# Expert slot tiles: the chosen expert's weights copied to fixed places by VectorE and ScalarE, and held stationary by TensorE

## The chip, the cores and the metric

The kernel runs on one core of a Trainium2 chip. The metric is the device time of one execution in microseconds; a kernel's time is the median of its runs. TensorE multiplies matrices, VectorE (DVE), ScalarE (ACT) and GpSimd (POOL) work elementwise, SyncE (SP) issues most transfers. Each engine has a queue of its own and works through it in order; semaphores tie the queues together.

## The reference

One block of a network, on x of 16 x 512 rows of 128 values: a modulated layer norm, a gather convolution whose result is added to x, a second modulated layer norm, and a mixture of 8 experts of which each row takes 2. The change touches only the experts:

```python
scores = jnp.einsum('btd,ed->bte', x, gate_w)
topk_scores, topk_idx = jax.lax.top_k(scores, TOP_K)       
topk_probs = jax.nn.softmax(topk_scores, axis=-1)
h12 = jnp.einsum('btd,ehd->bteh', x, w12)
h1, h2 = (h12[..., :H], h12[..., H:])
hidden = jax.nn.silu(h1) * h2
expert_out = jnp.einsum('bteh,edh->bted', hidden, w3)
y = jnp.sum(total_probs[..., None] * expert_out, axis=-2)
```

All data are float32.

## The kernel before

The kernel has two long stages. In the first (to about 1048 us) the convolution runs over 512 tiles, and each row's two experts are chosen. Each row, with its target and its gate, is scattered by GpSimd into a table in DRAM in which every expert has its own region, filled up to whole tiles of 128 rows. A table of tiles (`whichi`: the expert of each slot tile; `wherei`: where its rows stand) is worked out by VectorE.

The second stage runs over `SLOT_TILES` = 135 slot tiles, each of 128 rows of one expert. For tile j:

- SyncE loads the rows to `xt` (a ring of 12), L451.
- TensorE `slots_turned(j)` turns them, L1122, and VectorE `slots_out(j)` copies the result to `xT` (2 buffers), L1434.
- TensorE `hidden(j)`, L1128: one product with `xT` stationary and the expert's 512 columns of `w12` moving, read at an address that a register gives. The rows of the slot tile are the partitions of the result `ps_h`.
- ScalarE `silu(j)`, L852, on the first 256 columns; VectorE `hidden(j)`, L1440, multiplies by the other 256 and writes `hid`.
- TensorE `hidden_turned(j)`, L1135: two transposes, since the second product needs the inner dimension on the partitions; ScalarE `hidden_out(j)`, L858, copies them out to `hidT`.
- TensorE `second(j)`, L1143: two products (halves of the inner 256) with `hidT` stationary and the expert's `w3` moving, at an address from a register; each float32 product is two instructions.
- ScalarE `rows_out(j)`, L865, multiplies by the gate; VectorE `targets(j)`, L1447, converts the target indices; GpSimd scatters the rows to DRAM, L704, over a ring of 4.

The order is written out by hand. TensorE goes through `slots_turned(j + 2)`, `hidden(j + 1)`, `hidden_turned(j)`, `second(j - 1)`; VectorE through `slots_out(j + 2)`, `hidden(j + 1)`, `targets(j)`; ScalarE through `silu(j + 1)`, `hidden_out(j)`, `rows_out(j - 1)`. Nearly all buffers between them are double. Once in four tiles TensorE's queue (and SyncE's, for `wherei`) loads four numbers from SBUF into registers, L1154 (L445): one load instruction, then register arithmetic and an assertion for each number. After the last tile each row's two expert rows are fetched, added and stored with x.

Of the kernel before, what the change touches and what calls it, by code (L numbers as in the profile page):

```python
# [4 lines left out]
B, L, C = 16, 512, 128  # L5
HEADS, D, TAPS, BINS = 8, 16, 32, 64
P = 128
# [21 lines left out]
EXPERTS, FF = 8, 256  # L29
HALVES = FF // P  # L30
# [3 lines left out]
SLOT_TILES = ASSIGNED // P + EXPERTS - 1  # L34
SPARE = EXPERTS - 1
ROW = C + 2
XRING = 12
YRING = 4
EPS = 1e-5
MAX_FREQ, MIN_FREQ = 16.0, 1.0  # L40

# [51 lines left out]
def build(nc, x, wave_wT, wave_b, kern_wT, kern_b, out_wT, w12T, w3T, gateT, cT, wmod,  # L93
          c_n, c_p, c_e, c_tok, c_ident, c_iota, c_tri, c_id, c_trash, c_tile, out):
    fp32, bf16, i32, u32 = mybir.dt.float32, mybir.dt.bfloat16, mybir.dt.int32, mybir.dt.uint32
    ALU, ACT, AX = mybir.AluOpType, mybir.ActivationFunctionType, mybir.AxisListType
# [20 lines left out]
    with ctx:  # L117
        def sb(name, shape, dt=fp32):
            return ctx.enter_context(nc.sbuf_tensor(name, shape, dt))

        def pb(name):
            return ctx.enter_context(nc.psum_tensor(name, [P, 512], fp32))

        def sem(name):
            return ctx.enter_context(nc.semaphore(name))
# [5 lines left out]
        ident = sb("ident", [P, P])  # L131
# [75 lines left out]
        spots = sb("spots", [P, TOP, RES])  # L207
# [11 lines left out]
        whichi = sb("whichi", [P, SLOT_TILES + 1], i32)  # L219
# [7 lines left out]
        w12 = flat[:, 0:EXPERTS * 2 * FF]  # L227
        w3 = hgr[:, PAIRS % 2, :]
        xt = dl[:, :, :, :, :].rearrange("p s j h k -> p (s j h k)")[:, 0:XRING * ROW].rearrange("p (s n) -> p s n", s=XRING)
        zrow = att[:, :, :].rearrange("p a n -> p (a n)")[:, 0:EXPERTS * ROW].rearrange("p (e n) -> p e n", n=ROW)  # L230
        xT = ee[:, 0, 0:2 * P].rearrange("p (s n) -> p s n", s=2)
        sh = ee[:, 1, :].rearrange("p (s n) -> p s n", s=2)
        hid = aw[:, 0, 0:512].rearrange("p (s n) -> p s n", s=2)
        hidT = aw[:, 1, 0:512].rearrange("p (s n) -> p s n", s=2)
        yrow = aw[:, 2, 0:YRING * P].rearrange("p (s n) -> p s n", s=YRING)
        idu = sb("idu", [P, XRING], u32)
        y1 = att[:, 0:4, :].rearrange("p a n -> p (a n)").rearrange("p (s n) -> p s n", s=2)
# [5 lines left out]

        ps = [pb(f"ps{n}") for n in range(8)]
        ps_n, ps_p, ps_t, ps_y, side = ps[0:2], ps[2:4], ps[4:6], ps[6], ps[7]
        ps_x, ps_h, ps_u, ps_z = ps[0:2], ps[2:4], ps[4:6], ps[6:8]

        s_const, s_mod, s_modst, s_modld = sem("consts_loaded"), sem("mod_done"), sem("mod_stored"), sem("mod_loaded")
        s_silu, s_modps, s_zero = sem("silu_done"), sem("mod_product"), sem("edges_zeroed")
# [22 lines left out]
        s_w, s_spare, s_pad2, s_tab = sem("expert_weights_loaded"), sem("spare_filled"), sem("pad_spots_ready"), sem("tile_table_ready")  # L272
# [1 line left out]
        s_zrow = sem("zero_rows_ready")  # L274
        s_xt = [sem(f"slots_loaded{n}") for n in range(XRING)]
        s_xp, s_xe, s_hp, s_si, s_hid = sem("slots_turned"), sem("slots_evicted"), sem("hidden_product"), sem("silu_ready"), sem("hidden_ready")
        s_up, s_ue, s_zp, s_ze, s_idu = sem("hidden_turned"), sem("hidden_evicted"), sem("expert_product"), sem("expert_rows"), sem("targets_ready")
        s_ys = [sem(f"expert_scattered{n}") for n in range(YRING)]
        s_xf = [sem(f"pair_fetched{n}") for n in range(2)]
        s_xm = sem("kept_rows_loaded")  # L280
# [14 lines left out]
        def _(sp):  # L295
# [176 lines left out]
            for j in range(SLOT_TILES):  # L472
                slots_in(j)
                if j >= 2 * XRING and j - 2 * XRING < PAIRS:
                    kept_in(j - 2 * XRING)
            for n in range(YRING):
                sp.wait_ge(s_ys[n], 16 * len(range(n, SLOT_TILES, YRING)))
            fetch(0, 0)
# [9 lines left out]
        def _(pool):  # L488
            pool.memset(power[:, :], -0.5)
            pool.memset(middle[:, :], MIN_FREQ + (MAX_FREQ - MIN_FREQ) / 2)  # L490
            pool.memset(tiny[:, :], EPS)
            pool.memset(zeros, 0.0).then_inc(s_set, 1)
# [215 lines left out]
        def _(act):  # L708
# [100 lines left out]
            for T in range(NT):  # L809
                i, R, r, h = T // TILES, T // HEADS, T // HEADS % RES, T % HEADS  # L810
                last, more = i - 1, i + 1 < PAIRS
# [36 lines left out]
            def silu(j):  # L848
                act.wait_ge(s_hp, j + 1)
                if j >= 2:  # L850
                    act.wait_ge(s_hid, j - 1)
                act.activation(sh[:, j % 2, :], ps_h[j % 2][:, 0:FF], ACT.Silu).then_inc(s_si, 1)  # L852

            def hidden_out(j):
                act.wait_ge(s_up, j + 1)
                if j >= 2:
                    act.wait_ge(s_zp, j - 1)
                act.activation(hidT[:, j % 2, :], ps_u[j % 2][:, 0:FF], ACT.Copy).then_inc(s_ue, 1)  # L858

            def rows_out(j):  # L860
                s, y = j % XRING, j % YRING
                act.wait_ge(s_zp, j + 1)
                if j >= YRING:
                    act.wait_ge(s_ys[y], 16 * (j // YRING))
                act.activation(yrow[:, y, :], ps_z[j % 2][:, 0:C], ACT.Identity, scale=xt[:, s, C + 1:C + 2]).then_inc(s_ze, 1)  # L865

            silu(0)
            for j in range(SLOT_TILES):
                if j + 1 < SLOT_TILES:
                    silu(j + 1)  # L870
                hidden_out(j)
                if j:
                    rows_out(j - 1)
            rows_out(SLOT_TILES - 1)

        @block.tensor
        def _(pe):
# [188 lines left out]
            for T in range(NT):  # L1066
                i, R, r, h = T // TILES, T // HEADS, T // HEADS % RES, T % HEADS
                last, more = i - 1, i + 1 < PAIRS
# [54 lines left out]

            def hidden(j):
                pe.wait_ge(s_xe, j + 1)
                if j >= 2:
                    pe.wait_ge(s_hid, j - 1)
                nc.tensor.matmul(ps_h[j % 2][:, :], xT[:, j % 2, :], w12[:, bass.ds(experts[j % 8] * (2 * FF), 2 * FF)], start=True, stop=True).then_inc(s_hp, 1)  # L1128

            def hidden_turned(j):  # L1130
                pe.wait_ge(s_hid, j + 1)
                if j >= 2:
                    pe.wait_ge(s_ue, j - 1)
                for k in range(HALVES):
                    last = nc.tensor.transpose(ps_u[j % 2][:, k * P:k * P + P], hid[:, j % 2, k * P:k * P + P], ident[:, :])  # L1135
                last.then_inc(s_up, 1)

            def second(j):
                pe.wait_ge(s_ue, j + 1)
                if j >= 2:  # L1140
                    pe.wait_ge(s_ze, j - 1)
                for k in range(HALVES):
                    last = nc.tensor.matmul(ps_z[j % 2][:, 0:C], hidT[:, j % 2, k * P:k * P + P], w3[:, bass.ds(experts[j % 8] * (HALVES * C) + k * C, C)],  # L1143
                                            start=(k == 0), stop=(k == HALVES - 1))
                last.then_inc(s_zp, 1)

            experts = [None] * 8
            pe.wait_ge(s_tab, 1)
            pe.wait_ge(s_w, 32)
            pe.wait_ge(s_rk, PAIRS)  # L1150
            for j in range(-2, SLOT_TILES + 1):
                if (j + 2) % 4 == 0 and j + 2 < SLOT_TILES:
                    n = (j + 2) % 8
                    experts[n:n + 4] = nc.values_load_multi_w_load_instructions(whichi[0:1, j + 2:j + 6], engines=(mybir.EngineType.PE,),  # L1154
                                                                                min_val=0, max_val=EXPERTS - 1)[1]
                if j + 2 < SLOT_TILES:
                    slots_turned(j + 2)
                if 0 <= j + 1 < SLOT_TILES:
                    hidden(j + 1)
                if 0 <= j < SLOT_TILES:  # L1160
                    hidden_turned(j)
                if 0 <= j - 1 < SLOT_TILES:
                    second(j - 1)

        @block.vector
        def _(dve):
            n = [0]
# [175 lines left out]
            for T in range(NT):  # L1343
                i, R, r, h = T // TILES, T // HEADS, T // HEADS % RES, T % HEADS
                last, more = i - 1, i + 1 < PAIRS
# [68 lines left out]
            for k, d in enumerate((1, 2, 4)):  # L1414
                a, b = upto[:, k % 2, :], upto[:, 1 - k % 2, :]
# [14 lines left out]
            def slots_out(j):  # L1430
                dve.wait_ge(s_xp, j + 1)
                if j >= 2:
                    dve.wait_ge(s_hp, j - 1)
                nc.vector.tensor_copy(xT[:, j % 2, :], ps_x[j % 2][:, 0:P]).then_inc(s_xe, 1)  # L1434

            def hidden(j):
                dve.wait_ge(s_si, j + 1)
                if j >= 2:
                    dve.wait_ge(s_up, j - 1)
                nc.vector.tensor_tensor(hid[:, j % 2, :], sh[:, j % 2, :], ps_h[j % 2][:, FF:2 * FF], ALU.mult).then_inc(s_hid, 1)  # L1440

            def targets(j):
                s = j % XRING
                dve.wait_ge(s_xt[s], 16 * (j // XRING + 1))
                if j >= XRING:
                    dve.wait_ge(s_ys[j % YRING], 16 * ((j - XRING) // YRING + 1))
                nc.vector.tensor_copy(idu[:, s:s + 1], xt[:, s, C:C + 1]).then_inc(s_idu, 1)  # L1447

            slots_out(0)
            slots_out(1)  # L1450
            hidden(0)
            for j in range(SLOT_TILES):
                if j + 2 < SLOT_TILES:
                    slots_out(j + 2)
                if j + 1 < SLOT_TILES:
                    hidden(j + 1)
                targets(j)

            dve.wait_ge(s_xm, 16 * (3 * PAIRS - 1))
            for f in range(PAIRS):  # L1460
                s = f % 2
# [78 lines left out]
```

## Time and profile before

| | us |
|---|---|
| median of 3 runs | 1399.45 (1394.16 to 1401.42) |
| the profiled execution | 1404.66 |
| its span, first to last instruction | 1402.9 |
| TensorE matmuls busy over the span | 1131.3 (81%) |
| VectorE | 1037.9 (74%) |
| ScalarE | 931.3 (66%) |
| GpSimd | 711.3 (51%) |
| slot tiles: first slot transpose to last scatter | 1088.6 to 1353 |

Times in the profile are microseconds from the span's start, durations of single instructions often ns. PE is a matmul, PEld a weight load of TensorE, and a name with q at its end (PEldq, DVEq, ACTq) is the queue that feeds the engine: register work and waits are done there and are not counted as busy. "issue" is idle time for which the profile knows no other engine. The busy shares over the whole span say little here, since the two stages have different limits; the slot tiles are read by themselves.

### The profile page before, as it was taken

The page shows a single profiled execution, that of the slowest core. Times are in us where ns is not written, and L with a number is a line of the kernel's source. Part 1 is how long each engine was busy: PE and PEld are TensorE (multiplying, and loading weights), DVE is VectorE, ACT ScalarE, POOL GpSimd, SP SyncE. Part 2 cuts the span into 40 slices and gives each one's busy share as a digit, 9 for nine tenths or more (in the row PEclk, how much of TensorE's full clock was granted, in tenths as well). Part 3 has the DMA queues.
Part 4 walks back from the last instruction along what each step waited for, and adds up shares of the span by engine and source line. Part 5 has one row for each costly group of instructions (what it writes and reads, how often), then busy time and mean ns, then how long its engine had stood idle before and what let it go on. Part 6 is the DMA issues. An engine that isn't in the chain of part 4 may idle for free. (4 is left out here: it accounts for less than half of the span.)

```text
span 1402.9 us, 34813 instructions
## 1 busy us (share of the span) xinstructions
PE 1131.3 (81%) x11182; PEld 781.2 (56%) x11339; DVE 1037.9 (74%) x2314; ACT 931.3 (66%) x1905; POOL 711.3 (51%) x906
## 2 busy tenths in 40 slices
PE   0569998998999999899999989999930899999940
PEld 0346666665666666566666666666630565555530
DVE  1379899989989999998999999889933333333336
ACT  0268888788788878878887888788800455555530
POOL 4335227447745844854683584544336344545430
PEclk9989999999999999999999999999965899999975
DMA  4345445545544554554554455445511262222237
GB/s 160 112 127 151 140 105 157 154 127 152 154 125 133 171 135 129 156 146 115 171 149 124 133 143 135 140 133 136 155 57 42 73 191 71 71 71 73 67 119 266
DMA packets 213344, 181.27 MB, mean 129 GB/s; under 512 B 147632, under 2 KB 183344, under 8 KB 212272
## 3 DMA queue, kind: packets, MB, share of 16 engines
q1 hardware_dynamic: 204496, 161.12, 41.3%
q0 software_dynamic: 8672, 17.92, 3.8%
q8 instruction: 96, 1.57, 0.5%
q14 instruction: 80, 0.66, 0.2%
HBM read 96.86 MB, written 82.12 MB: 128 GB/s over the span
## 5 line engine op out<-in xcount | busy, mean ns | idle before, releaser
L774 ACT ACTIVATE ee<-ps,f 128x512 f32<-128x512 f32 x512 | 354.7, 693 | 120.1 <-remote 67.1
L1291 DVE TENSOR_TENSOR aw<-dq,ks 128x520 f32<-128x520 int32 x512 | 418.2, 817 | 2.2 <-DMA ks<-k_scratch 2.2
L1281 DVE SCALAR_TENSOR_TENSOR dq<-ps,ee 128x512 int32<-128x512 f32 x512 | 350.4, 684 | 45.4 <-PE ps L978 38.6
L986 PE MATMUL ps<-ident,aw 128*128 128x128 f32 x2048 | 314.6, 276 | 39.9 <-ACT att L782 22.5
L986 PEld LDWEIGHTS ps<-ident,aw 128*128 128x128 f32 x2048 | 239.0, 141 | 184.6 <-issue 66.2
L782 ACT ACTIVATE att<-ps 128x512 f32<-128x512 f32 x512 | 310.3, 606 | 20.7 <-PE ps L986 18.2
L978 PE MATMUL ps<-cn,ptt 128*128 128x512 bf16 x512 | 195.3, 382 | 28.3 <-issue 12.1
L614 POOL COPY kn<-kn 128x256 f32<-128x256 f32 x64 | 25.5, 398 | 348.9 <-DVE kn L1271 343.9
L704 POOL DMA_INDIRECT y_scratch<-aw,idu x135 | 129.6, 960 | 135.9 <-ACT aw L865 124.4
L583 POOL DMA_INDIRECT slot_scratch<-hrow,spotu x128 | 139.7, 1092 | 44.5 <-issue 33.4
L1440 DVE TENSOR_TENSOR aw<-ee,ps 128x256 f32<-128x256 f32 x135 | 56.9, 422 | 136.0 <-ACT ee L852 113.2
L852 ACT ACTIVATE ee<-ps 128x256 f32<-128x256 f32 x135 | 51.9, 384 | 156.7 <-PE ps L1128 144.2
L1128 PE MATMUL ps<-kn,ee 128*128 x270 | 143.5, 614 | 0.0
L1006 PE MATMUL ps<-att,dl 128*32 128x128 f32 x4096 | 138.4, 276 | 0.1
L973 PE MATMUL ps<-cp,ptt 128*128 128x512 bf16 x355 | 136.8, 385 | 0.2 <-issue 0.2
L1006 PEld LDWEIGHTS ps<-att,dl 128*32 128x32 f32 x4096 | 104.1, 109 | 21.7 <-ACT att L789 8.5
L993 PE MATMUL ps<-ident,ka 128*128 128x128 f32 x512 | 78.4, 276 | 17.0 <-POOL ka L628 15.9
L1122 PE MATMUL ps<-ident,dl 128*128 128x128 f32 x135 | 38.5, 285 | 60.7 <-issue 58.6
L621 POOL TENSOR_TENSOR kd<-kn 128x504 f32<-128x504 f32 x64 | 87.0, 1360 | 0.0
L789 ACT ACTIVATE att<-ps 128x512 f32<-128x512 f32 x128 | 77.2, 603 | 13.6 <-PE ps L993 13.5
L1143 PE MATMUL ps<-hgr,aw 128*128 x540 | 82.6, 275 | 0.2
L1135 PEld LDWEIGHTS ps<-ident,aw 128*128 128x128 f32 x270 | 38.2, 142 | 71.9 <-issue 62.1
(174 smaller groups left out, 1693.7 us busy)
## 6 DMA issues: line engine op xcount, KB each, us to landing
k_scratch<-kn SPq DMA_DIRECT2D x64, 512.0 KB, 3.4
ka<-e_scratch SPq DMA_DIRECT2D x64, 512.0 KB
ks<-k_scratch SPq DMA_DIRECT2D x128, 130.0 KB
e_scratch<-kr SPq DMA_DIRECT2D x128, 126.0 KB
dl<-slot_scratch SPq DMA_DIRECT2D x135, 65.0 KB
att<-y_scratch SPq DMA_DIRECT2D x16, 512.0 KB, 5.3
xc<-in_x SPq DMA_DIRECT2D x8, 512.0 KB, 5.9
h_scratch<-hx SPq DMA_DIRECT2D x16, 256.0 KB, 4.1
```

The costliest lines, as they stand in the source:

```text
L583: pool.indirect_dma_start(out=slots[:, :], out_offset=bass.IndirectOffsetOnAxis(ap=spotu[:, k * RES + r:k * RES + r + 1], axis=0), in_=hro ...
L621: pool.tensor_tensor(kd[:, R % 2, :].rearrange("p (h k) -> p h k", k=EDGES), k[:, :, LO:LO + EDGES], k[:, :, LO + 1:LO + BINS], ALU.subtra ...
L704: pool.indirect_dma_start(out=yscr[:, :], out_offset=bass.IndirectOffsetOnAxis(ap=idu[:, s:s + 1], axis=0), in_=yrow[:, y, :], in_offset=N ...
L774: act.activation(ee[:, T % ERING, :], ps_p[T % 2][:, :], ACT.Relu, scale=f27[:, i % 2, r, h:h + 1]).then_inc(s_e, 1)
L782: act.activation(att[:, h, :], ps_t[UNIT["tile", T] % 2][:, :], ACT.Copy).then_inc(s_ev, 1)
L973: nc.tensor.matmul(ps_p[T % 2][:, :], params_of(T), cp[:, T % QUAD, :], start=True, stop=True).then_inc(s_p, 1)
L978: nc.tensor.matmul(ps_n[T % 2][:, :], params_of(T), cn[:, T % QUAD, :], start=True, stop=True).then_inc(s_n, 1)
L986: last = nc.tensor.transpose(bank[:, j * P:j * P + P], aw[:, T % RING, o:o + P], ident[:, :])
L1006: last = nc.tensor.matmul(ps_y[ROWS * k:ROWS * k + ROWS, g * P:g * P + P], dl[:, R // RES % 2, j, h, :], att[:, h, j * P:j * P + P], start ...
L1128: nc.tensor.matmul(ps_h[j % 2][:, :], xT[:, j % 2, :], w12[:, bass.ds(experts[j % 8] * (2 * FF), 2 * FF)], start=True, stop=True).then_inc ...
L1281: nc.vector.scalar_tensor_tensor(dq[:, T % DRING, o:o + 512], ps_n[T % 2][:, :], SCALE, ee[:, T % ERING, :], ALU.mult, ALU.add).then_inc(s ...
L1291: nc.vector.tensor_tensor(aw[:, T % RING, :].rearrange("p (g k) -> p g k", k=8), dq[:, T % DRING, :].rearrange("p (g k) -> p g k", k=8), r ...
```

## The change

`w12c` (2 buffers of 512 columns) and `w3c` (2 of 256) are fixed places in SBUF. VectorE copies the tile's 512 columns of `w12` to the one (`first_weights`), ScalarE its 256 columns of `w3` to the other (`second_weights`). TensorE's `hidden` is now four products of 128 columns, each with a 128x128 block of `w12c` stationary and `xT` moving, so the result comes out with the inner dimension on the partitions. `hidden_turned` and `hidden_out` are gone; VectorE writes `hidT` (now 3 buffers) itself. The register loads move from TensorE's queue to VectorE's and ScalarE's.

The diff shows ScalarE first, then TensorE, then VectorE.

```diff
...
-            def hidden_out(j):
-                act.wait_ge(s_up, j + 1)
+            def second_weights(j):
+                if j % 4 == 0:
+                    spots[:] = nc.values_load_multi_w_load_instructions(whichi[0:1, j:j + 4], engines=(mybir.EngineType.Activation,),
+                                                                        min_val=0, max_val=EXPERTS - 1)[1]
                 if j >= 2:
                     act.wait_ge(s_zp, j - 1)
-                act.activation(hidT[:, j % 2, :], ps_u[j % 2][:, 0:FF], ACT.Copy).then_inc(s_ue, 1)
+                act.activation(w3c[:, j % 2, :], w3[:, bass.ds(spots[j % 4] * (HALVES * C), HALVES * C)], ACT.Copy).then_inc(s_w3, 1)
...
-            silu(0)
-            for j in range(SLOT_TILES):
+            act.wait_ge(s_tab, 1)
+            act.wait_ge(s_w, 32)
+            for j in range(-1, SLOT_TILES + 1):
                 if j + 1 < SLOT_TILES:
+                    second_weights(j + 1)
                     silu(j + 1)
-                hidden_out(j)
-                if j:
+                if j >= 1:
                     rows_out(j - 1)
-            rows_out(SLOT_TILES - 1)
...
             def hidden(j):
                 pe.wait_ge(s_xe, j + 1)
+                pe.wait_ge(s_w12, j + 1)
                 if j >= 2:
                     pe.wait_ge(s_hid, j - 1)
-                nc.tensor.matmul(ps_h[j % 2][:, :], xT[:, j % 2, :], w12[:, bass.ds(experts[j % 8] * (2 * FF), 2 * FF)], start=True, stop=True).then_inc(s_hp, 1)
+                for k in range(2 * HALVES):
+                    last = nc.tensor.matmul(ps_h[j % 2][:, k * P:k * P + P], w12c[:, j % 2, k * P:k * P + P], xT[:, j % 2, :], start=True, stop=True)
+                last.then_inc(s_hp, 1)
...
             def second(j):
-                pe.wait_ge(s_ue, j + 1)
+                pe.wait_ge(s_hid, j + 1)
+                pe.wait_ge(s_w3, j + 1)
                 if j >= 2:
                     pe.wait_ge(s_ze, j - 1)
                 for k in range(HALVES):
-                    last = nc.tensor.matmul(ps_z[j % 2][:, 0:C], hidT[:, j % 2, k * P:k * P + P], w3[:, bass.ds(experts[j % 8] * (HALVES * C) + k * C, C)],
+                    last = nc.tensor.matmul(ps_z[j % 2][:, 0:C], hidT[:, j % HRING, k * P:k * P + P], w3c[:, j % 2, k * C:k * C + C],
...
-                if (j + 2) % 4 == 0 and j + 2 < SLOT_TILES:
-                    n = (j + 2) % 8
-                    experts[n:n + 4] = nc.values_load_multi_w_load_instructions(whichi[0:1, j + 2:j + 6], engines=(mybir.EngineType.PE,),
-                                                                                min_val=0, max_val=EXPERTS - 1)[1]
                 if j + 2 < SLOT_TILES:
                     slots_turned(j + 2)
                 if 0 <= j + 1 < SLOT_TILES:
                     hidden(j + 1)
-                if 0 <= j < SLOT_TILES:
-                    hidden_turned(j)
                 if 0 <= j - 1 < SLOT_TILES:
                     second(j - 1)
...
+            def first_weights(j):
+                if j % 4 == 0:
+                    spots_of[:] = nc.values_load_multi_w_load_instructions(whichi[0:1, j:j + 4], engines=(mybir.EngineType.DVE,),
+                                                                           min_val=0, max_val=EXPERTS - 1)[1]
+                if j >= 2:
+                    dve.wait_ge(s_hp, j - 1)
+                nc.vector.tensor_copy(w12c[:, j % 2, :], w12[:, bass.ds(spots_of[j % 4] * (2 * FF), 2 * FF)]).then_inc(s_w12, 1)
+
             def hidden(j):
                 dve.wait_ge(s_si, j + 1)
-                if j >= 2:
-                    dve.wait_ge(s_up, j - 1)
-                nc.vector.tensor_tensor(hid[:, j % 2, :], sh[:, j % 2, :], ps_h[j % 2][:, FF:2 * FF], ALU.mult).then_inc(s_hid, 1)
+                if j >= HRING:
+                    dve.wait_ge(s_zp, j - HRING + 1)
+                nc.vector.tensor_tensor(hidT[:, j % HRING, :], sh[:, j % 2, :], ps_h[j % 2][:, FF:2 * FF], ALU.mult).then_inc(s_hid, 1)
...
-            slots_out(0)
-            slots_out(1)
-            hidden(0)
-            for j in range(SLOT_TILES):
+            dve.wait_ge(s_tab, 1)
+            dve.wait_ge(s_w, 32)
+            for j in range(-2, SLOT_TILES):
                 if j + 2 < SLOT_TILES:
+                    first_weights(j + 2)
                     slots_out(j + 2)
-                if j + 1 < SLOT_TILES:
+                if 0 <= j + 1 < SLOT_TILES:
                     hidden(j + 1)
-                targets(j)
+                if j >= 0:
+                    targets(j)
```

## Rows read from the trace of the kernel before

**Rows 1.** Stretches: length; busy us (instructions) by engine; PEclk; DMA; GB/s.

```profile
60.00:100.00 40.00, 27.05 (x194) 16.53 (x197) 24.69 (x52) 23.74 (x45) 11.56 (x22) 0.87 0.52 135
1150.00:1330.00 180.00, 163.53 (x847) 106.67 (x846) 66.91 (x282) 96.38 (x282) 90.34 (x95) 1.00 0.26 72
```

**Rows 2.** Chain of waits in the slot tiles: start us, us, what.

```profile
1202.59 0.11 PE ps L1122
1202.69 0.86 PE ps L1128 x2
1203.56 0.22 PE ps L1135 x2
1203.77 0.45 PE ps L1143 x4
1204.22 0.64 issue
1204.86 0.30 PE ps L1122
1205.16 1.05 PE ps L1128 x2
```

**Rows 3.** Register load on TensorE's queue, all, then one; the next weights.

```profile
L1154 PEldq TENSOR_LOAD <-whichi x34: 327/331/518, 1065.2 to 1340.7; - x34
...
L1154 PEldq FUSED_REGOPS  x4: 146/148/151, 1211.3 to 1212.2; - x4
L1154 PEldq SEQ_ASSERT  x4: 18/18/18, 1211.5 to 1212.4; - x4
L1154 PEldq TENSOR_LOAD <-whichi x1: 329/329/329, 1210.9 to 1210.9; - x1
...
1212.52 0.14 PEld L1122 LDWEIGHTS ps<-ident,dl 128*128 128x128 f32 x1 [0.92 <-issue]
```

**Rows 4.** Timeline of the slot tiles: start us, us, engine, line, operation.

```profile
1201.96 0.38 ACT L852 ACTIVATE ee<-ps 128x256 f32<-128x256 f32 x1 [0.60 <-issue]
1201.98 0.61 PE L1143 MATMUL ps<-hgr,aw 128*128 x4
1202.24 0.38 ACT L858 ACTIVATE aw<-ps 128x256 f32<-128x256 f32 x1
...
1202.38 0.42 DVE L1440 TENSOR_TENSOR aw<-ee,ps 128x256 f32<-128x256 f32 x1 [0.95 <-ACT ee L852]
...
1202.53 1.02 PE L1128 MATMUL ps<-kn,ee 128*128 x2
...
1202.71 0.15 DVE L1447 CAST idu<-dl 128x1 uint32<-128x1 f32 x1
1202.78 0.28 DVE L1434 COPY ee<-ps 128x128 f32<-128x128 f32 x1
...
1203.59 0.39 ACT L852 ACTIVATE ee<-ps 128x256 f32<-128x256 f32 x1 [0.60 <-PE ps L1128]
```

**Rows 5.** One-input VectorE work in SBUF, by line, then timeline beside a scatter.

```profile
L1409 DVE TENSOR_SCALAR fill<-filli 128x8 f32<-128x8 int32 x1 | 0.2, 172 | 0.0
...
1064.19 0.96 POOL L583 DMA_INDIRECT slot_scratch<-hrow,spotu  x1 [0.30 <-issue]
1064.22 0.23 DVE L1426 TENSOR_SCALAR which<-which 128x136 f32<-128x136 f32 x1
1064.75 0.43 DVE L1428 CAST wherei<-where 128x136 int32<-128x136 f32 x1
```

**Rows 6.** Semaphore waits on ScalarE's and VectorE's queues, 1150 to 1300 us.

```profile
L851 ACTq EVENT_SEMAPHORE  x79: 17/17/17, 1151.1 to 1299.6; - x79
L1439 DVEq EVENT_SEMAPHORE  x79: 21/21/21, 1152.1 to 1299.7; - x79
```

**Rows 7.** Timeline, GpSimd: one scatter of a row of them, idle time before.

```profile
1078.11 0.96 POOL L698 DMA_INDIRECT slot_scratch<-att,padu  x1 [0.30 <-issue]
```

More of the change, by code:

```diff
@@ L38 @@
 YRING = 4
+HRING = 3
 EPS = 1e-5
@@ L232, in build @@
         sh = ee[:, 1, :].rearrange("p (s n) -> p s n", s=2)
-        hid = aw[:, 0, 0:512].rearrange("p (s n) -> p s n", s=2)
-        hidT = aw[:, 1, 0:512].rearrange("p (s n) -> p s n", s=2)
+        hidT = aw[:, 0:2, :].rearrange("p a n -> p (a n)")[:, 0:HRING * FF].rearrange("p (s n) -> p s n", s=HRING)
+        w12c = ee[:, 2:4, :]
+        w3c = kr[:, :, :].rearrange("p s n -> p (s n)")[:, 0:2 * HALVES * C].rearrange("p (s n) -> p s n", s=2)
         yrow = aw[:, 2, 0:YRING * P].rearrange("p (s n) -> p s n", s=YRING)
@@ L245, in build @@
         ps_n, ps_p, ps_t, ps_y, side = ps[0:2], ps[2:4], ps[4:6], ps[6], ps[7]
-        ps_x, ps_h, ps_u, ps_z = ps[0:2], ps[2:4], ps[4:6], ps[6:8]
+        ps_x, ps_h, ps_z = ps[0:2], ps[2:4], ps[6:8]
         s_const, s_mod, s_modst, s_modld = sem("consts_loaded"), sem("mod_done"), sem("mod_stored"), sem("mod_loaded")
@@ L276, in build @@
         s_xp, s_xe, s_hp, s_si, s_hid = sem("slots_turned"), sem("slots_evicted"), sem("hidden_product"), sem("silu_ready"), sem("hidden_ready")
-        s_up, s_ue, s_zp, s_ze, s_idu = sem("hidden_turned"), sem("hidden_evicted"), sem("expert_product"), sem("expert_rows"), sem("targets_ready")
+        s_w12, s_w3, s_zp, s_ze, s_idu = sem("first_weights_copied"), sem("second_weights_copied"), sem("expert_product"), sem("expert_rows"), sem("targets_ready")
         s_ys = [sem(f"expert_scattered{n}") for n in range(YRING)]
@@ L852, in silu @@
                 act.activation(sh[:, j % 2, :], ps_h[j % 2][:, 0:FF], ACT.Silu).then_inc(s_si, 1)
-            def hidden_out(j):
-                act.wait_ge(s_up, j + 1)
+            spots = [None] * 4
+            def second_weights(j):
+                if j % 4 == 0:
+                    spots[:] = nc.values_load_multi_w_load_instructions(whichi[0:1, j:j + 4], engines=(mybir.EngineType.Activation,),
+                                                                        min_val=0, max_val=EXPERTS - 1)[1]
                 if j >= 2:
                     act.wait_ge(s_zp, j - 1)
-                act.activation(hidT[:, j % 2, :], ps_u[j % 2][:, 0:FF], ACT.Copy).then_inc(s_ue, 1)
+                act.activation(w3c[:, j % 2, :], w3[:, bass.ds(spots[j % 4] * (HALVES * C), HALVES * C)], ACT.Copy).then_inc(s_w3, 1)
             def rows_out(j):
@@ L1125, in hidden, with second @@
                 pe.wait_ge(s_xe, j + 1)
+                pe.wait_ge(s_w12, j + 1)
                 if j >= 2:
                     pe.wait_ge(s_hid, j - 1)
-                nc.tensor.matmul(ps_h[j % 2][:, :], xT[:, j % 2, :], w12[:, bass.ds(experts[j % 8] * (2 * FF), 2 * FF)], start=True, stop=True).then_inc(s_hp, 1)
-            def hidden_turned(j):
+                for k in range(2 * HALVES):
+                    last = nc.tensor.matmul(ps_h[j % 2][:, k * P:k * P + P], w12c[:, j % 2, k * P:k * P + P], xT[:, j % 2, :], start=True, stop=True)
+                last.then_inc(s_hp, 1)
+            def second(j):
                 pe.wait_ge(s_hid, j + 1)
-                if j >= 2:
[L1133 to L1138, printed above, removed]
-                pe.wait_ge(s_ue, j + 1)
+                pe.wait_ge(s_w3, j + 1)
                 if j >= 2:
@@ L1142, in second @@
                 for k in range(HALVES):
-                    last = nc.tensor.matmul(ps_z[j % 2][:, 0:C], hidT[:, j % 2, k * P:k * P + P], w3[:, bass.ds(experts[j % 8] * (HALVES * C) + k * C, C)],
+                    last = nc.tensor.matmul(ps_z[j % 2][:, 0:C], hidT[:, j % HRING, k * P:k * P + P], w3c[:, j % 2, k * C:k * C + C],
                                             start=(k == 0), stop=(k == HALVES - 1))
                 last.then_inc(s_zp, 1)
-            experts = [None] * 8
-            pe.wait_ge(s_tab, 1)
-            pe.wait_ge(s_w, 32)
             pe.wait_ge(s_rk, PAIRS)
             for j in range(-2, SLOT_TILES + 1):
-                if (j + 2) % 4 == 0 and j + 2 < SLOT_TILES:
-                    n = (j + 2) % 8
-                    experts[n:n + 4] = nc.values_load_multi_w_load_instructions(whichi[0:1, j + 2:j + 6], engines=(mybir.EngineType.PE,),
-                                                                                min_val=0, max_val=EXPERTS - 1)[1]
                 if j + 2 < SLOT_TILES:
@@ L1434, in slots_out @@
                 nc.vector.tensor_copy(xT[:, j % 2, :], ps_x[j % 2][:, 0:P]).then_inc(s_xe, 1)
+            spots_of = [None] * 4
+            def first_weights(j):
[5 more added lines that the diff above has]
+                nc.vector.tensor_copy(w12c[:, j % 2, :], w12[:, bass.ds(spots_of[j % 4] * (2 * FF), 2 * FF)]).then_inc(s_w12, 1)
             def hidden(j):
                 dve.wait_ge(s_si, j + 1)
-                if j >= 2:
-                    dve.wait_ge(s_up, j - 1)
-                nc.vector.tensor_tensor(hid[:, j % 2, :], sh[:, j % 2, :], ps_h[j % 2][:, FF:2 * FF], ALU.mult).then_inc(s_hid, 1)
+                if j >= HRING:
+                    dve.wait_ge(s_zp, j - HRING + 1)
+                nc.vector.tensor_tensor(hidT[:, j % HRING, :], sh[:, j % 2, :], ps_h[j % 2][:, FF:2 * FF], ALU.mult).then_inc(s_hid, 1)
             def targets(j):
```

## The prediction

> **What bounds the kernel now.** I first read the page's slices for stages. The last quarter of the span but for its end is a stage of its own: TensorE almost full, VectorE mostly idle. That is the loop over the 135 slot tiles, the only part the change touches. In its middle 180 us [rows 1] TensorE is busy 163.53 us (91%), with its clock granted in full (1.00, so the 2.4 GHz level); ScalarE 54%, VectorE 37%, GpSimd 50%. So TensorE bounds the stage, and what it does in each tile is the price list.
>
> The chain of waits gives that list [rows 2]: after the slot transpose (L1122, issued every 0.11 us) come 0.86 us of the wide product (L1128), 0.22 of two transposes back (L1135), 0.45 of the second product (L1143, four instructions, thus 0.112 each): 1.64 us a tile. Once in four tiles stands "issue", 0.64 us, followed by a slower start (0.30 and 1.05 where 0.11 and 0.86 are usual). This is the loading of four expert numbers into registers (L1154): the load instruction starts at 1210.9, and the next weights go in at 1212.52, 1.62 us later [rows 3]. It began while older matmuls still ran, hence only some 1.1 us show. From one load to the last one there are 17 groups in 1340.7 - 1210.9 = 129.8 us: **7.64 us for four tiles**, 1.91 each. Everything below is compared with this 7.64; there are 135/4 = 33.75 groups.
>
> **The change part by part.** *TensorE, throughput.* The wide product of 0.86 becomes four products of 128 columns. Each one is two instructions, as in L1143, so 8 x 0.112 = 0.90 us. The two transposes (0.22) go, and so does the register load (1.1 per group). A tile needs 0.11 + 0.90 + 0.45 = 1.46 us; if TensorE stayed the bound, a group took 5.84 us.
>
> *ScalarE.* It drops the eviction of the transposed rows (L858, 128x256, next instruction 0.28 us later) and gains a copy of the same 128x256 from SBUF. No row has that exact copy; between 0.24 and 0.34, I take 0.28 as the nearest [rows 4]. Busy time is unchanged, but the *order* is new. The copy for tile k waits for the second product of tile k-2 (its buffer), and the silu of tile k is queued right behind it. TensorE runs that second product after the hidden product of tile k. So silu(k), which now starts 0.04 us after its own product's end (1202.53 + 1.02 to 1203.59, [rows 4]), would then also wait for 0.45 us of other matmuls and a copy.
>
> *VectorE.* It gains a 128x512 f32 copy from SBUF. The nearest rows: in SBUF a one-input operation took 231 ns for 136 elements (L1426), against 172 for 8 (L1409), so 0.46 ns an element [rows 5]. That gives 172 + 504 x 0.46 = 404 ns; I take 0.40 from its start to the next one. At the slope of two-input work (0.33 for 256, L1440) it would be 0.60, the upper bound; 0.30 is the lower one. The copy for k+2 is queued behind hid(k), the product with the gate, and ahead of the transposed slots of k+2, and TensorE needs both of these before H(k+2).
>
> These two queues close a **loop** over two tiles. Its terms, with starts to next starts from [rows 4] and [rows 2], the first worked out above: H(k) 0.90; second product of k-2 0.45, its drain 0.16 (0.61 in the timeline less 0.45); hand-over to ScalarE 0.04; weight copy 0.28; silu 0.38; hand-over 0.04; hid(k) 0.33; targets 0.07; copy of the first weights 0.40; slots out 0.29; hand-over to TensorE 0.04 (taken like the others). Sum **3.38 us for two tiles**, 1.69 each. So TensorE with its 1.46 is no longer the bound even without any load; a group is 6.76 us.
>
> *The register load, moved.* Both VectorE and ScalarE now do it once in four tiles. On ScalarE it follows the scaled rows of k-3, and silu(k) waits anyway for a product that VectorE's own load has held up; more than 1.6 us of waiting covers it, and I cost it at nothing. If that cover were gone, it would show once per group as on VectorE. On VectorE it has no cover: it stands between targets and the weight copy, inside the loop. The queue runs ahead of the engine, so the load starts when hid(k) is released, about 0.15 us after it (two waits, two instructions); without a load the copy would start 0.33 + 0.07 = 0.40 after it. Its own length: 1.62 on TensorE's queue. VectorE's queue is slower: the same semaphore instruction takes 21 ns there against 17 on ScalarE's [rows 6]. With that ratio on all but the 0.33 of the load proper, 0.33 + 1.29 x 1.24 = 1.93. I take 1.85, nearer to the row of its own queue. Exposed: 0.15 + 1.85 - 0.40 = **1.60 us per group**; bounds 0.9 (a load of 1.15, the bare sum of the instructions' times in [rows 3], 0.33 + 4 x 0.166 = 0.99, plus some dispatch) and 2.0.
>
> The Trainium skill (Advanced Engine Details and Errata, Clock Domains) gives VectorE's sequencer 0.96 GHz and the others 1.2 GHz; the 21 and 17 ns agree with it. By that rule alone the load would be 1.62 x 1.25 = 2.03 us and the forecast some 6 us longer; the sum above rests on the rows.
>
> **Sum.** A group: 2 x 3.38 + 1.60 = 8.36 us against 7.64, so 0.72 x 33.75 = 24.3 us more. The profiled execution took 1404.66 us (span 1402.9 and what lies around it), so it would take 1429; this execution was 5 above the median of the three runs, 1399.45, and from that median the forecast is 1399.45 + 24.3 = **1424 us**. Nothing ahead of the stage changes: the first slot transpose waits for the scatters, which follow each other every 1.26 us until after 1078 [rows 7], while TensorE's first load stands at 1065.2 [rows 3], behind its wait for the weights: they are there, and the first copies will be. Break-even is an exposed load of 7.64 - 6.76 = 0.88 us.
>
> GpSimd's scatter needs 0.96 + 0.30 = 1.26 us [rows 7], under 2.1 a tile, so it has room. The DMA queues see the same transfers.
>
> **The rivals.**
> (a) *The load costs little on VectorE.* With 0 exposed a group takes 6.76, so -30 us: 1370; with 0.4 it is 1383. For: nobody has measured it on that queue. Against: [rows 3], and the load has no cover of more than 0.4. 0.12.
> (b) *TensorE remains the bound* (group 5.84): -61 us, 1339. For: 91% busy today. Against: silu(k) stands behind a wait for a product that TensorE runs later. It needs the loop's terms to be some 14% shorter and no load. 0.05.
> (c) *The copy of the first weights runs at one element per cycle* (0.60 instead of 0.40): twice 0.20 in each group's loop, +13.5 us: 1437. It decides if the rate of [rows 5] doesn't hold for a copy whose source address is in a register. 0.12.
> (d) *The copy and the scatter get in each other's way* in SBUF. L1428, 136 elements, took 0.43 us where L1426 took 0.23; it ended 0.03 after the scatter that had begun at 1064.19, while L1426 ran inside the same scatter undisturbed [rows 5]. If each copy in the loop loses that 0.20, +13.5 us: 1437. If it waits for half a scatter of 0.96, 0.48 x 2 x 33.75 = +32 us: 1456. 0.11 in all.
> The Trainium skill (SBUF - State Buffer, Who interferes with whom) says that a VectorE copy of this kind and a GpSimd instruction hold a shared port for their whole length, the second one fully blocked. That is the case with 1456; L1426's undisturbed 0.23 speaks against it, L1428's 0.43 for a part of it.
> (e) *TensorE's clock falls.* It would be busy 1.46 of 2.09 us, 70%. In 60 to 100 us of the span it was 68% busy and the clock granted was 0.87 [rows 1]. By that, a quarter of the time at the lower level adds some 0.39 to the 1.51 us of TensorE in the loop: +26 us, 1450. Pauses of over 0.6 us exist today at a full clock. 0.06.
>
> **How the numbers follow.** The forecast 0.49; (a) 0.12, (b) 0.05, (c) 0.12, (d) 0.11, (e) 0.06; the loop as said but the exposed load near break-even (0.7 to 1.1) 0.05. A measurement of this kernel can tell about 0.5%, 7 us, from no change. Faster by more than that: (a) and (b), 0.17. Within it: the last case and the short end of the forecast, 0.10. Slower: 0.73. The forecast's own range is 1400 to 1440: the load's bounds give -24 and +13, the two copies' lower ends -6 and -3. The range for 8 in 10 reaches over (c), most of (d) and (e), down to the near end of (a): 1392 to 1450.
>
> **What would show it.** In the profile after: TensorE about 70% busy in the stage; a group of four tiles 8.4 us long, with intervals between hidden products that alternate (about 1.46 and 1.92) and one of about 3.5; silu's idle time ended by the weight copy's wait, thus by the second product; VectorE's copy at 0.43; L1154's load gone from TensorE's queue and one of 1.8 to 2.0 us on VectorE's. Wrong if silu starts at its own product's end, if the copy takes 0.7 or varies with the scatter, if the idle time of TensorE is under 10%, or if the granted clock is under 1.

## The result, and the profile after

| | before | after |
|---|---|---|
| median of 4 runs each, us (before: the three above and one more) | 1400.06 | 1433.96 (1427.91 to 1435.38) |
| the profiled execution, us | 1404.66 | 1434.57 |
| slot tiles, first to last scatter, us | 253.7 | 288.5 |

The changed kernel is slower: ratio 1.0255, 95% interval 1.0223 to 1.0287. On another chip, that of the second set of experiments below, the kernel before took 1378 us and the changed one 1.0216 times as long (1.0199 to 1.0233). The slot tiles (start of the first scatter to start of the last: 1098.73 to 1352.40 before, 1093.55 to 1382.05 after) took 34.8 us more. The two profiled executions lie 29.9 us apart, since the stage ahead of the slot tiles ended some 5 us earlier in the second one; what made it do so stays open. On the other chip the kernel before with a short load and the changed kernel reach their first scatter at nearly the same time (1073.7 and 1074.3 us), so it doesn't look like a part of the change.

The same stretch as in [rows 1], of the kernel after: length; busy us (instructions) of PE, PEld, DVE, ACT, POOL; granted clock; DMA; GB/s.

```profile
1150.00:1330.00 180.00, 136.38 (x1080) 126.22 (x1079) 87.70 (x336) 78.74 (x250) 89.44 (x84) 0.97 0.22 63
```

TensorE fell from 163.53 to 136.38 us of the 180, and no other engine is above half. So no engine's own work fills the stage, and the waits have to be read. The longest waits of 1150 to 1350 us say which (engine and line, what it waited for: us in total, times, the longest):

```profile
ACT kr L865 <- PE ps L1146: 111.1, 88, 4.4
...
DVE aw L1445 <- ACT ee L854: 72.5, 68, 3.2
```

The first is ScalarE's copy of the second weights (L865) waiting for the second product (L1146); the silu (L854) behind it has no idle time of its own. That is the wait that the forecast named. The timeline lets the loop be read off, from one hidden product (L1137) to the next but one:

```profile
1199.80 1.16 PE L1137 MATMUL ps<-ee 128*128 128x128 f32 x8 [1.69 <-issue]
...
1200.80 0.61 PE L1146 MATMUL ps<-kr,aw 128*128 128x128 f32 x4
...
1201.35 1.06 PE L1137 MATMUL ps<-ee 128*128 128x128 f32 x8
1201.54 0.42 ACT L865 ACTIVATE kr<-hgr 128x256 f32 x1 [2.46 <-PE ps L1146]
1201.86 0.37 ACT L854 ACTIVATE ee<-ps 128x256 f32<-128x256 f32 x1
...
1202.26 0.42 DVE L1445 TENSOR_TENSOR aw<-ee,ps 128x256 f32<-128x256 f32 x1 [1.46 <-ACT ee L854]
...
1202.60 0.15 DVE L1452 CAST idu<-dl 128x1 uint32<-128x1 f32 x1
...
1202.66 0.42 DVE L1439 COPY ee<-kn 128x512 f32 x1
1202.76 1.15 POOL L706 DMA_INDIRECT y_scratch<-aw,idu  x1 [2.38 <-DVE idu L1452]
...
1202.99 0.28 DVE L1428 COPY ee<-ps 128x128 f32<-128x128 f32 x1
...
1203.33 1.16 PE L1137 MATMUL ps<-ee 128*128 128x128 f32 x8 [0.37 <-DVE ee L1428]
```

1199.80 to 1203.33 is 3.53 us for two tiles. The next round holds VectorE's register load; here the copy of the first weights (L1439) comes 1.72 us after hid (L1445) instead of 0.40:

```profile
1204.88 1.06 PE L1137 MATMUL ps<-ee 128*128 128x128 f32 x8
...
1205.79 0.42 DVE L1445 TENSOR_TENSOR aw<-ee,ps 128x256 f32<-128x256 f32 x1 [1.06 <-ACT ee L854]
...
1207.51 0.43 DVE L1439 COPY ee<-kn 128x512 f32 x1 [1.23 <-issue]
...
1208.18 1.16 PE L1137 MATMUL ps<-ee 128*128 128x128 f32 x8 [1.69 <-issue]
```

From 1199.80 to 1208.18 is a group of four tiles: **8.38 us**. The load itself, on VectorE's queue (shortest, median and longest duration in ns; first and last start):

```profile
L1435 DVEq FUSED_REGOPS  x4: 183/186/190, 1206.3 to 1207.1; - x4
L1435 DVEq SEQ_ASSERT  x4: 23/23/23, 1206.5 to 1207.3; - x4
L1435 DVEq TENSOR_LOAD <-whichi x1: 345/345/345, 1205.9 to 1205.9; - x1
```

One more thing differs from before: stretches at TensorE's lower clock level. Two neighbouring windows of 10 us, and from the chain of waits the eight matmuls of a hidden product (0.89 us at the full clock, when nothing holds them up) in such a stretch:

```profile
1190.00:1200.00 10.00, 7.94 (x53) 7.46 (x54) 4.09 (x18) 3.79 (x12) 3.88 (x4) 0.84 0.20 55
1200.00:1210.00 10.00, 7.94 (x68) 7.47 (x68) 5.00 (x20) 3.87 (x13) 4.66 (x5) 1.00 0.23 66
```

```profile
1189.82 2.07 PE ps L1137 x8
```

### The profile page after: what moved, and what is told of

Same layout as the page of the kernel before. It is cut to its first block, busy times and chain, and to the rows that moved or that the text cites. A ratio compares the mean times of both kernels' runs of the same rounds, so it can differ in the third digit from the quotient of the medians.

```text
span 1432.8 us, 36095 instructions
## 1 busy us (share of the span) xinstructions
PE 1136.2 (79%) x11879; PEld 835.3 (58%) x11879; DVE 1082.1 (76%) x2449; ACT 919.3 (64%) x1905; POOL 726.0 (51%) x906
## 4 chain that ended last, share of the span: by engine, by line
PE 47%; issue 13%; DVE 10%; ACT 5%; POOL 4%; DMA 2%; DVEq 1%; SPq 1%; another core or an unknown queue 1%; ACTq 0%; POOLq 0%
PE ps L993 9%; PE ps L1137 9%; PE ps L1013 5%; PE ps L980 5%; DVE aw L1285 4%; PE ps L985 4%; PE ps L1146 3%; PE ps L1000 2%; PE ps L1035 2%; PE ps L947 2%; PE ps L1023 2%; DMA att<-y_scratch 2%; DVE dq L1275 1%; ACT att L784 1%; ACT ee L776 1%
## 5 line engine op out<-in xcount | busy, mean ns | idle before, releaser
L993 PEld LDWEIGHTS ps<-ident,aw 128*128 128x128 f32 x2048 | 239.5, 141 | 182.7 <-issue 66.3
L706 POOL DMA_INDIRECT y_scratch<-aw,idu x135 | 143.0, 1059 | 156.8 <-DVE idu L1452 130.5
L1137 PE MATMUL ps<-ee 128*128 128x128 f32 x1080 | 157.2, 291 | 68.4 <-issue 44.0
L980 PE MATMUL ps<-cp,ptt 128*128 128x512 bf16 x512 | 197.3, 386 | 0.0
L1137 PEld LDWEIGHTS ps<-ee 128*128 128x128 f32 x1080 | 138.2, 200 | 84.6 <-issue 55.1
L865 ACT ACTIVATE kr<-hgr 128x256 f32 x135 | 56.2, 416 | 178.1 <-PE ps L1146 158.0
L1445 DVE TENSOR_TENSOR aw<-ee,ps 128x256 f32<-128x256 f32 x135 | 56.6, 419 | 111.6 <-ACT ee L854 109.2
L1439 DVE COPY ee<-kn 128x512 f32 x135 | 60.1, 445 | 43.3 <-issue 43.3
L1146 PE MATMUL ps<-kr,aw 128*128 128x128 f32 x540 | 84.8, 281 | 0.9 <-ACT aw L872 0.9
```

The lines of the kernel that those rows point to most:

```text
L706: pool.indirect_dma_start(out=yscr[:, :], out_offset=bass.IndirectOffsetOnAxis(ap=idu[:, s:s + 1], axis=0), in_=yrow[:, y, :], in_offset=N ...
L980: nc.tensor.matmul(ps_p[T % 2][:, :], params_of(T), cp[:, T % QUAD, :], start=True, stop=True).then_inc(s_p, 1)
L993: last = nc.tensor.transpose(bank[:, j * P:j * P + P], aw[:, T % RING, o:o + P], ident[:, :])
L1137: last = nc.tensor.matmul(ps_h[j % 2][:, k * P:k * P + P], w12c[:, j % 2, k * P:k * P + P], xT[:, j % 2, :], start=True, stop=True)
L1146: last = nc.tensor.matmul(ps_z[j % 2][:, 0:C], hidT[:, j % HRING, k * P:k * P + P], w3c[:, j % 2, k * C:k * C + C], start=(k == 0), stop=( ...
```

## The experiments

My theory: two lengthenings put the loop above TensorE's work, ScalarE's order (silu behind the weight copy, thus behind another tile's second product) and VectorE's register load, which has no cover. The rivals: the copies and GpSimd's scatters hold each other up; the eight products are the bound; the clock.

They ran in two sets, on two chips. The first set holds the runs without VectorE's load, without ScalarE's load, with silu first and with the shorter load on VectorE; the second set holds the changed kernel and the last three. Each is compared with the kernel before on its own chip (1378.32 us in the first set, 1377.87 in the second). Differences to the changed kernel, for runs of the first set, go by way of these two, which agree within 0.5 us.

### The changed kernel on another chip

> The changed kernel as it is, on the chip of these runs. Its slot stage took 288.4 us from first to last scatter in the first profile, 34.7 more than before: 25 by the longer groups (8.38 against 7.64) and about 10 by stretches with the TensorE clock at its lower level. If those stretches belong to the kernel: 34 over the kernel before again. If they belong to that chip or execution: 24 to 27 over it.

Measured: 1407.89 us, 30.0 over before, ratio 1.0216 (1.0199 to 1.0233). That is between the two answers. (The changed kernel ran on the chip of the second set only, not on that of the first.) The profile still shows lowered stretches, but fewer, for instance:

```profile
1190.00:1200.00 10.00, 7.95 (x56) 7.71 (x56) 3.84 (x16) 3.41 (x11) 4.21 (x4) 0.83 0.22 56
```

Of the ten-microsecond windows from 1080 to 1350 two are under 1.00 here. In the first profile six windows from 1130 to 1350 are at 0.93 or lower. Its slot stage is 282.6 us (1074.3 to 1356.9), 5.9 less than there, with the same 8.38 for an undisturbed group.

### Without VectorE's register load

```diff
-                if j % 4 == 0:
-                    spots_of[:] = nc.values_load_multi_w_load_instructions(whichi[0:1, j:j + 4], engines=(mybir.EngineType.DVE,), ...
...
-                nc.vector.tensor_copy(w12c[:, j % 2, :], w12[:, bass.ds(spots_of[j % 4] * (2 * FF), 2 * FF)]) ...
+                nc.vector.tensor_copy(w12c[:, j % 2, :], w12[:, 0:2 * FF]) ...
```

> Leaves out VectorE's register loads: every tile's first weights are copied from expert 0's place, at a fixed address; the amount copied is the same. Loop theory (two tiles of ScalarE's and VectorE's queues bound the stage, the load is exposed 1.32 us once in four tiles): a group of four falls from 8.38 to 7.06 us, 45 us less than the changed kernel (1434), so 1389; if the groups at a lowered TensorE clock also go, up to 10 less, 1379. Rival, the scatter and the copies hold each other up: the copies stay, so at most 10 us are won, 1424. Rival, the eight products of TensorE are the bound: no change, 1434.

Measured: 1361.94 us, 16.4 under before (ratio 0.9883, 0.9866 to 0.9899), thus 46 under the changed kernel; 45 had been expected from the load alone. The timeline:

```profile
1202.31 1.16 PE L1137 MATMUL ps<-ee 128*128 128x128 f32 x8 [0.35 <-DVE ee L1428]
...
1205.84 1.16 PE L1137 MATMUL ps<-ee 128*128 128x128 f32 x8 [0.36 <-DVE ee L1428]
...
1209.36 1.16 PE L1137 MATMUL ps<-ee 128*128 128x128 f32 x8 [0.35 <-DVE ee L1428]
```

Every round is now 3.53 or 3.52 us, a group 7.05. All copies were still there, and the products too. So the copies and the eight products by themselves don't make the kernel slower than before; it took the load on top. "Silu first", below, shows that it took the order on ScalarE as well: without either one, the kernel is faster than before.

### Without ScalarE's register load

```diff
-                if j % 4 == 0:
-                    spots[:] = nc.values_load_multi_w_load_instructions(whichi[0:1, j:j + 4], engines=(mybir.EngineType.Activation,), ...
...
-                act.activation(w3c[:, j % 2, :], w3[:, bass.ds(spots[j % 4] * (HALVES * C), HALVES * C)], ACT.Copy) ...
+                act.activation(w3c[:, j % 2, :], w3[:, 0:HALVES * C], ACT.Copy) ...
```

> Leaves out ScalarE's register loads: every tile's second weights are copied from expert 0's place. Loop theory: the load is hidden behind ScalarE's wait for the second product, so no change, 1434 within 5. Rival, it is exposed like VectorE's: 1.3 x 33.75 = 44 us less, 1390.

Measured: 1401.73 us, 23.4 over before (1.0175, 1.0158 to 1.0192); the changed kernel is 30.0 over it, so 6 to 7 us were won and not 44. In this order of the queue the load is hidden. Most of the little that was won is another term: with a fixed address the copy starts 0.04 us after the second product's end (1201.91 + 0.61 to 1202.56) instead of 0.13 (1200.80 + 0.61 to 1201.54 above).

```profile
1201.91 0.61 PE L1143 MATMUL ps<-kr,aw 128*128 128x128 f32 x4
```

```profile
1202.56 0.42 ACT L862 ACTIVATE kr<-hgr 128x256 f32<-128x256 f32 x1 [2.08 <-PE ps L1143]
```

Its hidden products at 1200.92 and 1209.17 are one group apart, 8.25 us; 0.13 less in 33.5 groups is 4.4 us, and the slot stage is 4.5 us shorter than that of the changed kernel (278.1 against 282.6). The other 2 us are within the noise of the two comparisons.

### Silu first

```diff
                 if j + 1 < SLOT_TILES:
-                    second_weights(j + 1)
                     silu(j + 1)
+                    second_weights(j + 1)
```

> Only the order on ScalarE: silu(j + 1) ahead of the copy of the second weights of j + 1. Loop theory: silu no longer waits for the second product, 0.61 + 0.13 + 0.32 us leave the loop of two tiles; TensorE's 1.46 and VectorE's load are left, a group takes about 6.9 instead of 8.38, 49 us less than the changed kernel, 1385 (1375 if the clock stays up), under the kernel before. Rivals (copies and scatter in each other's way, eight products slow): 1420 or more.

Measured: 1357.61 us, 20.7 under before (0.9858, 0.9841 to 0.9874) and about 50 under the changed kernel, where 49 was expected. Two lines changed places, and a kernel slower than before became one 1.4% faster:

```profile
1199.91 1.16 PE L1137 MATMUL ps<-ee 128*128 128x128 f32 x8 [0.58 <-DVE ee L1428]
...
1201.46 1.06 PE L1137 MATMUL ps<-ee 128*128 128x128 f32 x8
...
1202.91 1.06 PE L1137 MATMUL ps<-ee 128*128 128x128 f32 x8
...
1204.52 1.16 PE L1137 MATMUL ps<-ee 128*128 128x128 f32 x8
...
1206.82 1.16 PE L1137 MATMUL ps<-ee 128*128 128x128 f32 x8 [0.59 <-DVE ee L1428]
```

A group is 6.91 us. The loop of 3.53 is gone (1.55, 1.45, 1.61), and one interval of 2.30 is left in a group. VectorE's load stands in it, but not alone. With silu ahead of it, ScalarE's load (L861) has lost its cover: the chain of waits of this kernel runs through both loads. In this order of the queue ScalarE's load delays its weight copy, thus the scaled rows (L872) and the next silu (L854), and by them the hid behind which VectorE's own load starts:

```profile
1201.46 0.15 ACTq L861
...
1202.14 0.15 ACTq L861
...
1202.79 0.26 ACT aw L872
1203.05 0.37 ACT ee L854
...
1204.52 0.35 DVEq L1435
```

How much of the 6.91 each load makes wasn't measured by itself; with both of them short, in the last experiment, a group is 5.80.

### A shorter load on VectorE

```diff
                     spots_of[:] = nc.values_load_multi_w_load_instructions(whichi[0:1, j:j + 4], engines=(mybir.EngineType.DVE,),
-                                                                           min_val=0, max_val=EXPERTS - 1)[1]
+                                                                           min_val=0, max_val=EXPERTS - 1,
+                        skip_runtime_bounds_check_because="which is clamped to EXPERTS - 1 and starts at 0")[1]
```

> VectorE's register loads without the bounds assertions, so with less register arithmetic behind the load instruction; all else as in the changed kernel. Loop theory with the length in the arithmetic (4 x 0.3 us of 1.6): the exposed part falls from 1.3 to 0.4 to 0.6, a group to 7.5 to 7.7, 23 to 30 us less, 1404 to 1411. Rival, the length is in the load instruction and its latency: under 8 us less. Rival theories without the load in the loop: 1434.

Measured: 1367.8 us, 10.5 under before (0.9933, 0.9917 to 0.995) and 40 under the changed kernel, more than the 23 to 30 expected. Of the load's line only one kind of instruction is left in the queue:

```profile
L1435 DVEq TENSOR_LOAD <-whichi x34: 340/345/597, 1045.6 to 1305.8; - x34
```

The four blocks of register arithmetic went with the assertions. The expectation had part of them stay. In the timeline the copy comes 0.59 us after hid (1203.97 to 1204.56), against 0.40 without a load, so 0.2 of 1.3 us is left exposed:

```profile
1203.97 0.42 DVE L1445 TENSOR_TENSOR aw<-ee,ps 128x256 f32<-128x256 f32 x1 [1.06 <-ACT ee L854]
...
1204.56 0.43 DVE L1439 COPY ee<-kn 128x512 f32 x1
```

### The idle time of TensorE filled

```diff
             def hidden(j):
+                if j >= 4 and j % 4 == 0:
+                    for k in range(12):
+                        nc.tensor.transpose(ps[4 + k % 2][:, 0:P], ident[:, :], ident[:, :])
                 pe.wait_ge(s_xe, j + 1)
```

> The changed kernel with 12 transposes more once in four tiles (of the identity into unused PSUM, results not used), placed where TensorE idles about 1.7 us for VectorE's register load; about 1.3 us of it is filled. Loop theory: the loop isn't longer, nor shorter. If idle time brings the clock down, the lower stretches go, up to 10 us less than the changed kernel beside it, group 8.38 throughout; if the changed kernel shows none on this chip, no change. Rival, TensorE's own time bounds the stage: 1.3 x 33.75 = 44 us more.

Measured: 1406.8 us (ratio 1.0213, 1.0196 to 1.023), 1.1 under the changed kernel beside it. With 1.3 us of work more in each group the kernel takes the same time: TensorE's own work is not the bound, and that rival is out. The filler filled the gap (its 12 transposes, then the next hidden product 0.37 us after their end):

```profile
1209.45 1.47 PE L1134 MATMUL ps<-ident 128*128 128x128 f32 x12
1211.30 1.16 PE L1140 MATMUL ps<-ee 128*128 128x128 f32 x8 [0.37 <-DVE ee L1431]
```

The clock was 1.00 in every window from 1080 to 1350, as in this one:

```profile
1190.00:1200.00 10.00, 8.89 (x78) 8.42 (x77) 4.78 (x20) 3.98 (x13) 5.26 (x5) 1.00 0.23 63
```

The slot stage is 280.6 us, which is 33.5 groups of 8.38, against 282.6 for the changed kernel with its two lowered stretches. So some 2 us were to be won on this chip, and the 1.1 measured are within the noise. The lower level also shows in the run without ScalarE's load (0.89, 0.94 and 0.83 in three windows), which has the pauses of 1.7 us too. In the other experiments no window that lies wholly within the slot tiles, from 1080 us on, is under 1.00. That the pauses bring the clock down fits these profiles, but filling them was measured in one profile only, and its gain in time isn't clear of noise.

### The kernel before with a short load

The same edit as for VectorE above, on TensorE's load (L1154) in the kernel before.

> The kernel before, its register loads on TensorE's queue without the bounds assertions. The load then costs TensorE between 0 and 0.3 instead of 1.1 us in four tiles: a group of 6.6 to 6.9 instead of 7.64, 25 to 35 us less than before. Rival, the load instruction's own latency keeps most of it: under 10 us less.

Measured: 1343.99 us, 33.9 under before (ratio 0.9756, 0.974 to 0.9773). Its hidden products:

```profile
1200.49 1.02 PE L1128 MATMUL ps<-kn,ee 128*128 x2
1202.12 1.02 PE L1128 MATMUL ps<-kn,ee 128*128 x2
...
1207.03 1.02 PE L1128 MATMUL ps<-kn,ee 128*128 x2
```

The two products that the cut leaves out start at 1203.76 and 1205.39. That makes 6.54 us for four tiles with no gap, four times the 1.64 of [rows 2]. The whole cost of the load has gone, not by moving it but by shortening it.

### Silu first, both loads short

> The changed kernel with silu ahead of the copy of the second weights and both register loads without assertions. Loop theory: both terms that made the loop longer than TensorE's work are gone, TensorE's 1.46 us a tile bounds the stage, a group of 5.85 to 6.2: 49 to 60 us less than the kernel before. Rival, GpSimd's scatter, lengthened by the copies to 1.15 + 0.30 = 1.45 us, bounds it at nearly the same 5.8, which the waits would show. Rival, the copies and the queues of VectorE cost more when all run closer: 6.6 or more, 35 or less.

Measured: 1323.47 us, 54.4 under before (ratio 0.9608, 0.9592 to 0.9624), the fastest of all. The chain of waits in the stage is TensorE alone:

```profile
1180.44 0.45 PE ps L1146 x4
1180.89 0.11 PE ps L1129
1181.00 0.89 PE ps L1137 x8
1181.89 0.45 PE ps L1146 x4
```

1.45 us a tile, a group of 5.80. The waits from 1100 to 1260 us, below, show GpSimd idle for 53.6 of the 160 us, so the scatter doesn't bound it. Only here does the change pay what TensorE's sum promised: against the kernel before with a short load it is 20.5 us faster, near (6.54 - 5.80) x 33.5 = 24.8. At this pace a new wait appears, 3.2 us for the loads of the slot rows, all of it between 1105 and 1121 us; that is most of what is missing:

```profile
POOL y_scratch L706 <- ACT aw L872: 53.6, 98, 2.3
PEld ps L1129 <- DMA dl<-slot_scratch: 3.2, 3, 1.7
```

## Why the prediction was right, and where its terms were off

Forecast: 24.3 us slower, 1424 us, with 1392 to 1450 as the range; measured 33.9 slower, 1433.96 us, and 30.0 slower on the other chip. The mechanism and its place were as said. That the size of a group came out within 0.02 us is partly luck, since two errors cancel in it. The rest of the difference is the group of before, taken 0.07 us too long, and the clock, taken as full.

**The bound moves off TensorE into a loop of two queues.** Right. TensorE 76% busy in the stage (70 was forecast); silu behind the weight copy's wait. "Silu first" took the order away and won 50 us.

**The loop's terms.** 3.53 us against 3.38. From product to second product 1.00 instead of 0.90: after a wait for VectorE the weight load starts no earlier than the first matmul (both at 1203.33), where it is 0.11 us ahead of it in a full queue (1201.24 and 1201.35), and the forecast used that pace. The hand-over to ScalarE 0.13 instead of 0.04, since register arithmetic for the address stands behind the wait (46 to 51 ns on L865's queue); with a fixed address it was 0.04. The weight copy on ScalarE 0.32 against 0.28. Against these, VectorE's copy took 0.33 instead of 0.40: the next instruction starts before its end, as the two-input rows had shown. The forecast had two rounds 0.30 too short.

**The register load.** The exposed part was 1.32 us, not 1.60, so 0.28 too long. The ratio between the queues was right for the arithmetic (186 ns against the 148 of [rows 3], 1.26, where the semaphores gave 1.24), but I applied it to the whole 1.29 behind the load, gaps included, and the whole took no longer than on TensorE. The sequencer clocks of the Trainium skill (Advanced Engine Details and Errata, Clock Domains), 0.96 and 1.2 GHz, are 1.25 to one, which agrees with the single instructions here. The 2.03 us that the forecast worked out from them for the whole load, an estimate, didn't come. The two errors cancel: two rounds 0.30 too short and a load 0.28 too long, 8.38 measured against 8.36.

**ScalarE's load at nothing.** Right within what can be told, for this order of the queue: without it the groups are 0.13 shorter, which the hand-over of 0.04 instead of 0.13 in each of two rounds is enough to explain. It isn't free as such: with silu first it stands in the chain of waits.

**The group of before.** 7.64 was read off the last 17 groups. From first to last scatter (134 tiles, 33.5 groups) 253.7 us make 7.57. That is 0.07 x 33.5 = 2.4 us that the forecast lacks.

**The clock, rival (e).** Given 0.06, and partly true: the groups of 8.38 explain (8.38 - 7.57) x 33.5 = 27 of the 34.8 us in the first profile. The rest lies in a few groups of 9.3 to 10.4 us, which hold stretches at the lower level; there the eight matmuls take up to 2.07 instead of 0.89. The forecast treated the clock as all or nothing. Against the filled run's stage of 280.6 us it is some 8 us in one profile and some 2 in the other. Among the signs of being wrong the forecast had a granted clock under 1, and that sign came (0.97 in the stage), without the loop being wrong: it was too strict a sign. The load of 1.8 to 2.0 us on VectorE's queue didn't come either; it was 1.6.

**The other rivals.** (a) and (b) fell with the load's 1.32 and the loop's 3.53. (c) fell: 0.42 to 0.43 us for 512 elements with no scatter in the way, the rate of [rows 5]. (d) fell as a bound, though copy and scatter do lengthen each other. The scatter of 1202.76, with a copy begun just ahead of it, took 1.15 us instead of 0.96, and the copy its usual 0.42. In the changed kernel's first profile 25 of the 135 copies, all begun 0.54 to 0.89 us into a scatter, took 0.52 to 0.64, as here:

```profile
1199.35 1.02 POOL L706 DMA_INDIRECT y_scratch<-aw,idu  x1 [0.49 <-ACT aw L872]
...
1200.06 0.55 DVE L1439 COPY ee<-kn 128x512 f32 x1
```

Nothing waited for that copy: TensorE's next hidden product, at 1201.35, had no idle time before it, and GpSimd had time to spare. Copies begun earlier in a scatter weren't held up, as this one of the run "silu first":

```profile
1203.42 0.97 POOL L706 DMA_INDIRECT y_scratch<-aw,idu  x1 [2.00 <-ACT aw L872]
...
1203.85 0.42 DVE L1439 COPY ee<-kn 128x512 f32 x1
```

The Trainium skill (SBUF — State Buffer, Who interferes with whom) states that a VectorE copy in a mode with two ports and a GpSimd instruction share a port pair, and that the first of them holds it for its whole length while the other is fully blocked. These rows don't show such a lock: the copy at 1203.85 ran inside a scatter and took no longer than others. The case with 1456 us didn't come.

## What to carry to other kernels

Before adding work to an idle engine, write down the loop that its queue order closes: an engine that is less than half busy can still set the pace, if what is queued behind the new instruction is what the busiest engine needs. Put the instruction whose result is needed later behind the one whose result is needed sooner; here two lines in the other order were worth some 50 us. And before moving a stall to another queue, look at what it is made of: most of the register load was a bounds assertion's arithmetic, and dropping it, with the values clamped beforehand (L1426), won 33.9 us in the kernel before, with nothing moved. A cover that hides a load belongs to one order of the queue, too: read it again when the order changes.

## What the runs showed of the hardware that I had not expected

- Loading four numbers with assertions costs 1.6 us on VectorE's queue as on TensorE's. Without them 0.2 is exposed on VectorE, none on TensorE: 33.9 us over 34 loads of a kernel of 1378.
- TensorE, 76% busy from 1150 to 1330 us with a pause of 1.7 us in every group, kept its full clock for most of the stage and lost it in a few short stretches, more of them in one profile (six windows of 10 us) than in the other (two). With the pauses filled, none in one profile.
- VectorE's 512-element copy in SBUF and GpSimd's indirect scatter mostly overlap. A scatter took up to 1.15 us instead of 0.96 when a copy had begun about 0.1 us ahead of it. With silu first, all 60 copies begun in the first 0.44 us of a scatter took 0.41 to 0.43; in the changed kernel, 21 copies begun 0.54 to 0.71 us into one took 0.52 to 0.64.
